# Routing stage of a fused attention and expert block: partial results added in pairs ahead of the output projection, and a third place in the row buffer

## What is computed

```python
x = x + tanh(g_xattn) * (attention(layernorm(x), ctx) @ Wo + bo)   # sparsemax attention
x2 = layernorm(x)                                                  # no learned scale
probs = softmax(x2 @ router_w)
top_p, top_e = top_k(probs, 2)
y = sum over the two k of top_p[k] * (gelu(x2 @ w_in[e_k] + b_in[e_k]) @ w_out[e_k] + b_out[e_k])
out = x + tanh(g_ffn) * y
```

## Time and profile before

| | |
|---|---|
| median of 3 runs | 7035.43 us |
| the profiled execution's own time | 7039.05 us |
| its span in the trace | 7037.1 us |
| TensorE busy, share of the span | 74% |
| VectorE | 85% |
| ScalarE | 80% |
| GpSimd | 35% |
| mean granted clock of TensorE, share of 2.4 GHz | 0.73 |

### The profile page before, as it was taken

How to read it: one execution, slowest core, us unless ns; L and a number is a source line. 1 busy time by engine, 2 the same in 40 slices (tenths; PEclk the granted TensorE clock), 3 DMA queues, 4 the chain that set the end, 5 groups by cost and what they waited for, 6 DMA issues and landing times. The chain is left out here.

```text
span 7037.1 us, 168443 instructions
## 1 busy us (share of the span) xinstructions
PE 5172.3 (74%) x20066; PEld 1710.6 (24%) x20067; DVE 5965.4 (85%) x50050; ACT 5620.4 (80%) x12612; POOL 2481.6 (35%) x10299
## 2 busy tenths in 40 slices
PE   8985776776777777676767777776777777779794
PEld 5551111111111111111111111111111111158573
DVE  4558999999999999999999999999999999945445
ACT  2327998998999999998999999989999999922231
POOL 2222333333333333333333333333333333323431
PEclk9996676776677666676666676766676676789897
DMA  5761111111111111111111111111111111154235
GB/s 194 237 205 44 31 31 30 32 31 29 31 32 31 31 31 31 30 29 31 31 28 30 32 33 31 32 30 28 34 32 31 34 32 32 25 183 176 90 100 187
DMA packets 370269, 417.56 MB, mean 59 GB/s; under 512 B 118688, under 2 KB 286240, under 8 KB 368672
## 3 DMA queue, kind: packets, MB, share of 16 engines
q1 hardware_dynamic: 355872, 370.61, 18.7%
q0 software_dynamic: 13056, 35.74, 1.4%
HBM read 249.13 MB, written 156.88 MB: 58 GB/s over the span
## 5 line engine op out<-in xcount | busy, mean ns | idle before, releaser
L871 DVE MAX8 a_cand<-a_scores 128x8 f32<-128x42 f32 (+1 forms) x38912 | 4386.0, 195 | 297.2 <-issue 255.3
L594 PE MATMUL a_ring<-a_q,a_k 99*128 99x512 bf16 (+1 forms) x3328 | 1470.1, 554 | 799.8 <-ACT a_scores L659 533.6
L624 ACT ACTIVATE a_junk_act<-a_cand,a_ntau 128x304 f32<-128x304 f32 (+1 forms) x3840 | 1932.2, 518 | 150.9 <-DVE a_ntau L733 65.4
L539 PE MATMUL a_out<-a_attn,a_v 128*16 128x512 f32 (+1 forms) x6656 | 1407.1, 787 | 524.2 <-ACT a_attn L663 524.0
L659 ACT COPY a_scores<-a_ring 128x1024 f32<-128x1024 f32 (+1 forms) x2048 | 1607.6, 827 | 205.9 <-DVEq L825 107.8
L663 ACT ACTIVATE a_attn<-a_ring 128x1024 f32<-128x1024 f32 (+1 forms) x1792 | 1653.1, 975 | 2.0 <-PE a_ring L594 1.6
L590 PE MATMUL a_ring<-a_k,a_q 96*128 96x512 bf16 (+1 forms) x4096 | 1345.4, 457 | 83.2 <-DVE a_ident L684 32.9
L624 ACT ACTIVATION_READ_ACCUMULATOR a_junk_act<-a_cand,a_ntau 128x1 f32 x3840 | 784.9, 204 | 0.0
L590 PEld LDWEIGHTS a_ring<-a_k,a_q 96*128 96x128 bf16 x4096 | 385.9, 117 | 1454.4 <-ACT a_attn L663 673.4
L594 PEld LDWEIGHTS a_ring<-a_q,a_k 99*128 99x128 bf16 (+1 forms) x3328 | 285.7, 118 | 1642.3 <-ACT a_scores L659 913.7
L539 PEld LDWEIGHTS a_out<-a_attn,a_v 128*16 128x16 f32 (+1 forms) x6656 | 136.4, 100 | 1203.3 <-ACT a_attn L663 755.5
(11 more groups left out here) (227 smaller groups left out, 6279.1 us busy)
## 6 DMA issues: line engine op xcount, KB each, us to landing
a_k<-k_parts SPq DMA_DIRECT2D x1536, 50.0 KB
k_parts<-p_ks SPq DMA_DIRECT2D x48, 800.5 KB, 7.4
o_parts<-a_o SPq DMA_DIRECT2D x1024, 32.0 KB, 1.6
e_o<-o_parts SPq DMA_DIRECT2D x64, 512.0 KB
p_ctx<-in_ctx_t SPq DMA_DIRECT2D x16, 1601.0 KB, 8.6
v_heads<-p_v SPq DMA_DIRECT2D x16, 1536.0 KB
a_q<-q_parts SPq DMA_DIRECT2D x1536, 16.0 KB
a_v<-v_heads SPq DMA_DIRECT2D x256, 96.0 KB
```

The lines of the kernel that those rows point to most:

```text
L539: mm = nc.tensor.matmul(out_ps[at:at + HEAD_DIM], v_st[0:rows, u, c], attn[0:rows, k, (c % 2) * BANK:(c % 2 + 1) * BANK], start=c < 4, sto ...
L594: mm = nc.tensor.matmul(at[0:rows, m * BANK:(m + 1) * BANK], k_st[0:SCORE_ROWS + TAU_ROWS, ut, c * P:c * P + rows], q_st[0:SCORE_ROWS + TA ...
L624: ins = nc.scalar.activation(into[:, t].rearrange("p (a b) -> p a b", b=CHUNKS), cand[:, u % SLOTS, t, 0:w], ACT.Relu, bias=ntau[:, u % 2, ...
L871: ins = V.max(cand[:, u % SLOTS, t, :, c], scores[:, u % SLOTS, t, lo:hi])
```

## The change

The row buffer `rows` and the destinations `place_i` get a third place: every use of them goes by b % 3, and every wait for the scatters of the batch that had the place goes to batch b - 3 in place of b - 2. Of the buffer `o_s` two places remain. VectorE gets one new instruction a batch, in `bias`: it waits for the load of the four partial results and adds results 1 and 3 to results 0 and 2, in place, 128 partitions by 2048 float32 elements. TensorE waits for that addition in place of the load, and multiplies the two sums alone: 16 matmuls a batch in place of 32.

```diff
+    DEPTH = 3
-        rows = sb("rows", [P, 2, NK, TILES, DIM + 1])
+        rows = sb("rows", [P, DEPTH, NK, TILES, DIM + 1])
-        place_i = sb("place_i", [P, 2, TILES, NK], I32)
+        place_i = sb("place_i", [P, DEPTH, TILES, NK], I32)
-        scattered = sems("scattered", 2)
+        scattered = sems("scattered", DEPTH)
+        paired = sem("paired")
...
             for b in range(BATCH):
-                u = b % 2
+                u = b % DEPTH
                 pool.wait_ge(placed, b + 1)
                 pool.wait_ge(copied, b + 1)
...
             def project(b):
                 u = b % 2
-                pe.wait_ge(o_loaded[u], 64 * (b // 2 + 1))
+                pe.wait_ge(paired, b + 1)
 
                 pe.wait_ge(x2_done, b)
                 for t in range(TILES):
-                    for s in range(4):
+                    for s in (0, 2):
                         for a in range(HALVES):
                             mm = nc.tensor.matmul(o_ps[:, t * DIM:(t + 1) * DIM], o_s[:, u, a, s, t * P:(t + 1) * P], wo_s[:, a],
-                                                  start=s == 0 and a == 0, stop=s == 3 and a == HALVES - 1, skip_group_check=True)
+                                                  start=s == 0 and a == 0, stop=s == 2 and a == HALVES - 1, skip_group_check=True)
                 mm.then_inc(projected, 1)
...
             def turn(b):
-                u = b % 2
+                u = b % DEPTH
...
-                if b >= 2:
-                    act.wait_ge(scattered[u], 16 * TILES * NK * (b // 2))
+                if b >= DEPTH:
+                    act.wait_ge(scattered[u], 16 * TILES * NK * (b // DEPTH))
...
             def bias(b):
                 u = b % 2
                 dve.wait_ge(x_loaded[u], 16 * (b // 2 + 1))
+                dve.wait_ge(o_loaded[u], 64 * (b // 2 + 1))
+                V.tensor_tensor(o_s[:, u, :, 0:4:2], o_s[:, u, :, 0:4:2], o_s[:, u, :, 1:4:2], ALU.add).then_inc(paired, 1)
                 link(V.tensor_tensor(x2[:, b], x2[:, b], bo_s[:].unsqueeze(1).broadcast_to([P, TILES, DIM]), ALU.add))
...
             def norm(b):
-                u = b % 2
+                u = b % DEPTH
...
-                if b >= 2:
-
-                    dve.wait_ge(scattered[u], 16 * TILES * NK * (b // 2))
+                if b >= DEPTH:
+
+                    dve.wait_ge(scattered[u], 16 * TILES * NK * (b // DEPTH))
```

More of the change, by code:

```diff
@@ L1152, in _ @@
             sp.wait_ge(pads_stored, 16 * EXPERTS)
-            for u in range(2):
-                sp.wait_ge(scattered[u], 16 * TILES * NK * BATCH // 2)
+            for u in range(DEPTH):
+                sp.wait_ge(scattered[u], 16 * TILES * NK * len(range(u, BATCH, DEPTH)))
             def load(j, u, g):
@@ L1232, in route @@
                     for t in range(TILES):
-                        mm = nc.tensor.transpose(turn_ps[:, a, t * P:(t + 1) * P], rows[:, b % 2, 0, t, a * P:(a + 1) * P], ident[:])
+                        mm = nc.tensor.transpose(turn_ps[:, a, t * P:(t + 1) * P], rows[:, b % DEPTH, 0, t, a * P:(a + 1) * P], ident[:])
                 mm.then_inc(turned, 1)
```

## The result

The changed kernel took 6965.20 us, the median of 5 runs (6964.22 to 6969.01), against 7035.43 us, which is also the median of the 5 runs of the kernel before made with it: a ratio of 0.9901, with a 95% interval from 0.9887 to 0.9916. That is 70.2 us, or 1.0%, faster; 75 us were forecast, and the time lies 4.8 us above the forecast. The profiled execution took 6964.22 us with a span of 6962.3.

The account below looks back on a forecast made before the run. VectorE's scatter loop and TensorE's projection loop both bound the routing stage; start 4.0, twelve steps of 19.71 - 14.85 = 58.3, and end 12.7 make 75 us off 7035.4: 6960.4 us, range 6944 to 6988.

Parts of the forecast that it names:

- Two loops within a microsecond: Routing stage before the change: VectorE's loop through the scatters and TensorE's projection loop nearly equal, at 19.7 us a step.
- VectorE's work of 14.15: VectorE's step without waits in the changed routing stage: 11.83 us of present work plus 2.3 for the addition.
- The projection at 9.1: TensorE's halved projection: 7.0 us at full clock plus a low-clock spell, 8.7 to 10.0, taken as 9.1.
- `moment` waits 0.7 us: VectorE's wait for the projection each step, since the loop through addition and projection takes 14.85 us against 14.15.
- The load of `o_s` hidden from the fourth batch on: The addition's load wait: none after batch 2, as the load takes about 10 us and is late only beyond 17.
- Start and end: Outside the twelve steady steps: first burst at 6266.5, 4.0 us sooner; last bursts follow GpSimd's pace, saving 12.7 us.
- the full clock throughout: Rival: projection takes 7.0 us and VectorE's 14.15 us of work binds; 6949 us, chance 0.12.
- The low clock in every projection: Rival: projections back at 14.06 us, route work at full clock, no steady gain; 7029 us, chance 0.05.
- the low clock all through: Rival: TensorE stays at 1.2 GHz for the whole stage and its 21.8 us loop binds; 7054 us, chance 0.04.
- The load as the wait: Rival: loading `o_s` takes 20 us and sets the loop, 16.4 us a step; 6979 us, chance 0.05.
- a third place without effect: Rival: scatters land late anyway, VectorE's wait for them stays, and the period is 21.1 us; chance 0.02.
- the 0.96 us a step that the prediction had set aside for VectorE: Port lock when an addition meets a scatter: VectorE could wait up to 0.96 us a step, 11.5 us worse in sum.

Follow-up runs that it names:

- one half: The third place in the row buffer alone, without the addition and with 32 matmuls a batch, against the kernel before: 7028.18 us, ratio 0.9987.
- the other: The addition and 16 matmuls a batch alone, with two places in the row buffer, against the kernel before: 7049.73 us, ratio 1.0019.
- the variant with added matmuls: Changed kernel plus five matmuls a step whose result nobody reads, placed where TensorE stood idle: 6955.20 us, ratio 0.9882 to the kernel before.
- the sooner addition: Changed kernel with batch b+1's addition moved ahead of batch b's mean and variance, 2.0 us sooner: 6954.44 us, ratio 0.9884 to the kernel before.
- both the sooner addition and the added matmuls: Changed kernel with the earlier addition and the five unread matmuls a step together: 6953.10 us, ratio 0.9882 to the kernel before.

## Why the prediction was right

By its own steps:

- **Two loops within a microsecond, so neither half is enough.** Shown: loops of 19.36 and 18.7 us; 8 us gained by one half, 13 us lost by the other, 70 gained by both.
- **The addition at 2.3 us.** Sixteen times 2.29, within 0.003 of each other.
- **VectorE's work of 14.15** (its two terms make 14.13). 13.94 to 13.98 in the steps that wait for nothing.
- **The projection at 9.1.** The average of the twelve in the steady part is 9.35, with 8.64 at the least and 10.22 at the most, where 8.7 to 10.0 was said. The term was mis-sized by 0.25, and that is what the twelve steps missed: a period of 15.05 in place of 14.85 is 2.4 us. There is a pattern in it that a mean hides, and that the forecast didn't foresee: one projection of 10.0 to 10.2 follows each one or two of 8.6 to 8.9.
- **`moment` waits 0.7 us.** It waits 0.97 a step.
- **The load of `o_s` hidden from the fourth batch on**, and the third batch's data at 6246: the addition of batch 2 starts at 6246.62.
- **Start and end.** First burst at 6266.16, forecast 6266.5; last at 6477.9, forecast 6476. The projections of batches 0 and 1 took 10.2 and 9.1 us, where 9.3 and 7.0 had been put down; it cost nothing, for the third batch's data came later still.
- **Sum.** 74.8 us between the two profiled executions, 75 forecast; 70.2 between the medians. The difference of 4.6 is that the profiled execution before was 3.6 over its median and the one after 1.0 under it. The forecast read 75 us from that slower execution and took them from the median, and that is most of the 4.8 us by which it missed. That 74.8 comes so close to 75 is partly luck: 1.3 us of it come from the stage before, and 1.6 from behind the last scatter. Without both it is 71.9 us.

The rivals: the full clock throughout was wrong for this kernel, and its price nearly right. It had been put 11 us under the forecast; the variant with added matmuls came 10 us under the changed kernel, at 6955, with a mean granted clock of 0.97. The low clock in every projection and the low clock all through didn't come: no steady projection took over 10.22 us, where 14.06 would be one without the full clock, and the mean of the steady part is 0.84. For the second of them the prediction had called on the Trainium skill ("TensorE: Matmul & The Clock Gate", section "Loop structure matters more than you think"). That section speaks of a long wait for DMA between every matmul, 8 us in its example. TensorE's longest wait in the steady part here was 1.4 us, so the prediction stretched it to a case that it doesn't describe. Part of the loss came all the same: the low clock costs this kernel 10 us. The load as the wait, and a third place without effect, fall by the waits shown at the head: 8.6 us in three batches, and none for the scatters.

An addition that meets a scatter cost nothing in the changed kernel. The prediction had the two side by side. In nine of the twelve steady steps the addition starts when the burst is over, and in three within the burst's last scatter (6306.26, 6381.35 and 6442.09); those three took 2.29 us like the others, and no scatter took over 1.23. So the 0.96 us a step that the prediction had set aside for VectorE didn't come, here or in any variant. Where the two do meet at a cost, GpSimd pays it, as is shown below.

## What to carry to other kernels

Where two loops share an engine and are nearly as long, look for the change that shortens both, and don't judge either half by its own run: here one half alone looks useless and the other harmful. When a piece of work moves to another engine and so gets a producer behind it, follow the new loop link by link and put the producer as early in its engine's order as its inputs allow; here putting it 2 us sooner brought 11 us, as much as taking away nearly all of the low clock. A TensorE phase that gets shorter while the stretch between such phases gets longer loses part of the gain to the clock: price it by the rows where the clock had already fallen.

## What the runs showed of the hardware that had not been expected

**A VectorE addition holds a scatter back, and not the other way.** With the sooner addition its start falls beside the end of a burst. From that variant's timeline:

```profile
6300.74 2.28 DVE L1364 TENSOR_TENSOR e_o<-e_o 128x2048 f32<-128x2048 f32 x1
6300.99 2.87 POOL L1201 DMA_INDIRECT xs<-e_rows,e_place_i  x1 [0.31 <-issue]
```

The scatter that began 0.25 us after the addition took 2.87 us in place of 0.96, and ended 0.84 after it. The mean of the 96 scatters of the steady part is 1.18 us against 0.96 in the changed kernel, 1.8 us a burst. The additions took 2.28 us each.

The other order is in the record too. These are three lines of the variant with both the sooner addition and the added matmuls:

```profile
6283.89 0.96 POOL L1201 DMA_INDIRECT xs<-e_rows,e_place_i  x1 [0.30 <-issue]
...
6283.94 2.28 DVE L1368 TENSOR_TENSOR e_o<-e_o 128x2048 f32<-128x2048 f32 x1
...
6285.16 1.90 POOL L1201 DMA_INDIRECT xs<-e_rows,e_place_i  x1 [0.30 <-issue]
```

The scatter that began 0.05 us ahead of the addition took its usual 0.96 us, and the addition its usual 2.28 beside it: neither waited. The next scatter, begun inside the addition, again ended 0.84 us after it. In the variant with the added matmuls alone the addition started inside a scatter in all twelve steady steps, and took 2.29 us each time. The Trainium skill (SBUF — State Buffer, section "SBUF: two separate sides") has the port pair of the two engines as an exclusive lock: a VectorE operation with two SBUF inputs and a GpSimd operation that reads SBUF contend for it, whichever starts first holds it for the whole instruction, and the other blocks. The runs agree where the addition is first. Where the scatter is first they show no block: no VectorE addition waited. Whether such a scatter still needs the ports by then, no run shows.

GpSimd had 4.5 us or more of slack a step in the changed kernel and has 2.2 or more in the variant with the sooner addition, so the longer scatters cost nothing.

**Matmuls whose result nobody reads can pay.** Five a step, some 2.2 us at the full clock in time that TensorE had stood idle, raised the mean granted clock of the steady part from 0.84 to 0.97, shortened the projections from 9.35 to 7.2 us in most steps, and brought 10 us.

**A delay ahead of a projection costs more than its length.** 1.3 us of VectorE work ahead of the addition made the step 1.9 us longer: the projections behind it took 9.93 us on average in place of 9.35. With the clock held up the same work cost 1.3 us in the eight steps where the projection took 7.17.
